# Indirect DMAs of 128 partitions in place of 125 in a two-layer graph network kernel

## The chip, the cores and the metric

One core of one Trainium2 chip. The metric is the device time of one execution in microseconds (us), the median of three runs.

## What is computed

Two layers on a graph of 12,500 nodes with 256 features and 212,500 edges, sorted by destination. The parts around the change are the two edge sums:

```
# layer 0: norm = dinv[src] * w * dinv[dst]
agg = segment_sum(norm[:, None] * h[src], dst, num_segments=12500)
# layer 1, with source and destination in exchanged roles
out = segment_sum(edge_vals[:, None] * seq_fts[edge_col], edge_row, num_segments=12500)
```

In both, each edge fetches a row of 256 floats (1 KB) by one end's index and adds it, weighted, to the row of the other end. Layer 1 sums by source, so the edges have to be put into another order first: every edge becomes a record of three words (12 B) and is written to its place in an array `sorted_recs`. Around the sums stand a linear attention, a mixture of eight experts (layer 0), a second attention with a feed-forward part and a slice attention (layer 1).

## The kernel before

Nodes are taken in 100 tiles of P = 125, edges in 1700 rows of 125. A plan stage (`plan`, L181) lays the edges of a layer out in 1800 steps of up to 125 edges, all of one tile; `k.src_p`, `k.dloc_p` and `k.w_p` hold for every step, one lane (partition) per edge, the row to fetch, the place in the tile and the weight. The plan fetches edge rows with indirect DMAs of its own, 120 lanes each (L288), and turns them with TensorE.

The edge sum is the class `Aggregation` (L840), used by `sum_layer0` (L959) and `sum_layer1` (L2046). Each layer goes through 25 supertiles of STEPS = 72 steps, in groups of GRP = 6. Per step:

- GpSimd (POOL) issues one indirect DMA, L885, that gathers 125 rows of 1 KB, one to a partition, into one of RING = 18 buffers (three groups). Before a group it waits until TensorE has finished the group three before (L881). Twice in a supertile it copies 36 columns of indices into `idx` (L873).
- VectorE builds a 125x125 matrix from place and weight, L916.
- TensorE multiplies matrix by rows, L950, into one of three PSUM buffers. It waits once per group for the six gathers (L946).
- VectorE adds the result to `k.sums`, L935.

Every engine runs its own instruction list in order; semaphores join them. Other work of a layer is written by hand into the same lists, between half groups of three steps: in layer 0 the keys of the attention and the ranks of the edges for the later order (DVE L1050, PE L1118, L1126); in layer 1 the attention and the feed-forward part. In layer 1 POOL also computes the two reciprocal roots of a supertile (`rstd`, L2155 and L2158), one ahead of the gathers of group 3, one ahead of those of group 7 (L2165 to L2168); each waits for VectorE's mean and variance.

`finish_layer0` (L1270) goes through 50 pairs of tiles. TensorE runs 32 slots of expert products per pair with the rest of the layer between them; POOL issues the scatter of the records, 34 indirect DMAs of 125 lanes x 12 B per pair (L1456), in four shares between four rstds (L1438, L1441), the last share of 17 ahead of the next pair's first rstd, which VectorE waits for at L1544. SP loads records and positions for the scatter from DRAM (L1415, L1416) and waits before for the scatters of an earlier pair (L1414).

POOL runs with no other queue for these DMAs: gathers and scatters, copies of indices and rstds stand in one list.

Of the kernel before, what the change touches and what calls it, by code (L numbers as in the profile page):

```python
# [23 lines left out]

P = 125
TS = 4
D = 256
# [153 lines left out]
def plan(nc, k, layer):  # L181
# [10 lines left out]
    with ExitStack() as ctx:  # L192
# [100 lines left out]
        def _(eng):  # L293
# [7 lines left out]

            eng.memset(ones[:], 1.0).then_inc(ones_done, 1)
            link(eng.memset(k.dloc_p[:, NS:], -1.0))
            link(eng.memset(k.w_p[:, NS:], 0.0))
# [52 lines left out]
            for g in range(NG):  # L357
                eng.wait_ge(edges_in[g], 16 * len(fetches))
                if g >= 2:

                    eng.wait_ge(turned, g - 1)
                eng.tensor_copy(src_f[:, g % 2, :], src_g[:, g, :])
                eng.tensor_copy(w_f[:, g % 2, :], w_g[:, g, :])
                eng.tensor_scalar(dst_f[:, g % 2, :], dst_g[:, g, :], ntile_col[:, g:g + 1], None, ALU.add)\
                   .then_inc(edges_f, 1)
                eng.wait_ge(turned, g + 1)
                for n, out in enumerate((k.src_p, k.dloc_p, k.w_p)):
                    eng.tensor_copy(out[:, g * SG:(g + 1) * SG], ps_t[0:P, n, (g % 2) * 256:(g % 2) * 256 + SG])\
                       .then_inc(laid, 1)
# [470 lines left out]
class Aggregation:  # L840
# [8 lines left out]
    def __init__(self, nc, k, sb, pb, sem, table):  # L849
        self.nc, self.k, self.table = nc, k, table  # L850
        self.idx = [sb(f"idx{n}", [P, STEPS // 2], I32) for n in range(2)]
        self.rows = sb("gathered", [P, self.RING, D])
        self.lay = sb("lay", [P, 2, GRP, P])
# [87 lines left out]
    def multiply(self, i, g, half):  # L941
# [5 lines left out]
        for l in range(half * GRP // 2, (half + 1) * GRP // 2):  # L947
            s = g * GRP + l
            eng.wait_ge(self.added, i * STEPS + s + 1)
            eng.matmul(self.res[s % self.RES][:, 0, :], self.lay[:, g % 2, l, :],  # L950
                       self.rows[:, s % self.RING, :], start=True, stop=True).then_inc(self.multiplied, 1)

# [317 lines left out]
def finish_layer0(nc, k):  # L1270
# [11 lines left out]
    with ExitStack() as ctx:  # L1282
# [42 lines left out]
        rs = sb("rstds", [P, 4, TE])  # L1325
        rec = sb("rec", [P, 2, RPP, 3], I32)
        pos = sb("pos", [P, 2, RPP], I32)
        ps_up = [pb(f"ps_up{n}", [128, TE * P]) for n in range(2)]
# [10 lines left out]
        x_in = [sem(f"x_in{j}") for j in range(TE)]  # L1339
        rec_in = [sem(f"rec_in{n}") for n in range(2)]  # L1340
        scattered = [sem(f"scattered{n}") for n in range(2)]
        out_done = [sem(f"out_done{j}") for j in range(TE)]
# [35 lines left out]
        def _(eng):  # L1378
# [24 lines left out]
            def run(i, n, turn, front=True, moe=True, back=True):  # L1403
# [7 lines left out]
                if moe:  # L1411

                    if not isinstance(i, int) or i > 0:
                        eng.wait_ge(S.share_done, i)  # L1414
                    eng.dma_start(rec[:, n, :, :], k.rec_d[:, bass.ds(i * RPP, RPP), :]).then_inc(rec_in[n], 16)  # L1415
                    eng.dma_start(pos[:, n, :], k.pos_d[:, bass.ds(i * RPP, RPP)]).then_inc(rec_in[n], 16)  # L1416
                if back:
# [11 lines left out]
        def _(eng):  # L1429
            eng.memset(neg_half[:], -0.5).then_inc(S.power_ready, 1)  # L1430
            eng.wait_ge(S.power_ready, 1)
            eng.sem_inc(S.share_done, 1)
# [1603 lines left out]
def whole(nc, **t):  # L3036
# [16 lines left out]
    with ExitStack() as ctx:  # L3053
# [13 lines left out]
        k.pos_d = nc.dram_tensor("pos_d", [P, k.ROWS], I32, kind="Internal").ap()  # L3067
        k.sorted_recs = nc.dram_tensor("sorted_recs", [E, 3], I32, kind="Internal").ap()
        k.sorted_rows = k.sorted_recs.rearrange("(r e) f -> r (e f)", e=P)

# [42 lines left out]
def step_lists(k, sb):  # L3113
    k.src_p = sb("src_p", [P, k.NS], I32)
    k.dloc_p = sb("dloc_p", [P, k.NS + GRP])
# [30 lines left out]
```

## Time and profile before

| | |
|---|---|
| median of 3 runs | 11389.68 us (11383.44 to 11391.83) |
| profiled execution: span | 11392.9 us, 3.2 us above the median |
| TensorE (PE) busy | 8144.0 us, 71% |
| POOL busy | 7159.8 us, 63% |
| VectorE (DVE) busy | 6467.8 us, 57% |
| mean granted TensorE clock | 0.795 of full |

The profile gives no time of its own for the profiled execution beside the span, from its first instruction to its last. Busy time does not hold register, branch, semaphore and DMA-issuing work of an engine's sequencer; for POOL's indirect DMAs the time in which it makes them is shown as busy, the time between two of them as idle, with "issue" as the releaser where nothing was waited for. An average over the span says little here, since the stages have different limits; the profile is cut at them below.

### The profile page before, as it was taken

Reading aid. Unit: us, or ns where it says so; the run is one execution under the profiler, and the core shown is the slowest. Engines: PE = TensorE matmul, PEld = TensorE weight load, DVE = VectorE, ACT = ScalarE, POOL = GpSimd, SP = SyncE. Lnnn points to the kernel's source line nnn. Section 1 sums busy time; section 2 is a strip of 40 time slices with the busy share of each in tenths; the row PEclk is TensorE's granted clock in tenths of the full one; section 3 lists DMA queues with packets and bytes.
Section 4 is the critical chain, followed back from the end, with each engine's and each line's share of the span. In section 5 each row is a group of like instructions: output and inputs, shape, how many; then the busy total and the mean of one; then the engine's idle time right before and its main releaser. Section 6 shows DMA issues by size and latency. Waiting matters only on the chain. (4 is left out here: it accounts for less than half of the span.)

```text
span 11392.9 us, 139911 instructions
## 1 busy us (share of the span) xinstructions
PE 8144.0 (71%) x33573; PEld 5854.9 (51%) x33573; DVE 6467.8 (57%) x21682; ACT 1705.4 (15%) x3275; POOL 7159.8 (63%) x6381
## 2 busy tenths in 40 slices
PE   4633666666666688888888876777778777777778
PEld 3422444444444466666666654545545455444446
DVE  5853666666666555555555545566665665544431
ACT  0000000000000133333333330000101000011100
POOL 2224777777777577777777776777777777500001
PEclk7656777787787788888888876888878888777779
DMA  1013333333333211111111113333333333222224
GB/s 44 23 48 98 87 90 88 90 88 90 90 88 90 51 17 17 16 16 16 16 16 16 16 15 86 86 87 86 86 88 86 88 86 86 72 64 62 63 75 140
DMA packets 751763, 731.65 MB, mean 64 GB/s; under 512 B 422416, under 2 KB 612397, under 8 KB 750777
## 3 DMA queue, kind: packets, MB, share of 16 engines
q0 software_dynamic: 529008, 487.89, 19.0%
q1 hardware_dynamic: 209539, 224.42, 6.3%
q10 hardware_dynamic: 12755, 15.35, 0.4%
q14 instruction: 436, 3.57, 0.1%
q8 instruction: 25, 0.41, 0.0%
HBM read 613.00 MB, written 108.35 MB: 63 GB/s over the span
## 5 line engine op out<-in xcount | busy, mean ns | idle before, releaser
L885 POOL DMA_INDIRECT sum_gathered<-table,sum_idx x3600 | 4403.9, 1223 | 1159.5 <-issue 1019.3
L950 PE MATMUL sum_agg_res<-sum_gathered,sum_lay 125*125 125x256 f32 x7200 | 2443.1, 485 | 1571.3 <-DMA sum_gathered<-table,sum_idx 964.1
L950 PEld LDWEIGHTS sum_agg_res<-sum_gathered,sum_lay 125*125 125x125 f32 x7200 | 1604.7, 237 | 2185.7 <-issue 1092.0
L1456 POOL DMA_INDIRECT sorted_recs<-fin_rec,fin_pos x1700 | 2117.7, 1246 | 504.0 <-issue 499.7
L935 DVE TENSOR_TENSOR all_sums<-all_sums,sum_agg_res 125x256 f32 x3600 | 1513.8, 421 | 1517.4 <-PE sum_agg_res L950 1364.7
L916 DVE TENSOR_SCALAR sum_lay<-all_lane,sum_dloc_now,sum_w_now 125x125 f32<-125x125 f32 x3612 | 1444.0, 403 | 20.8 <-DVE sum_xn_tiles L1067 17.3
L1887 PE MATMUL fin_ps_up<-fin_tokens_T,fin_w 128*128 128x250 f32 x3200 | 995.1, 447 | 0.0
L1895 PE MATMUL fin_ps_dn<-fin_w,fin_hidden 128*125 128x256 f32 x3200 | 860.3, 404 | 10.2 <-issue 10.0
L1887 PEld LDWEIGHTS fin_ps_up<-fin_tokens_T,fin_w 128*128 128x128 f32 x3200 | 695.9, 231 | 166.6 <-issue 69.2
L1525 DVE SCALAR_TENSOR_TENSOR fin_acc<-fin_ps_dn,fin_comb,fin_acc 125x256 f32<-125x256 f32 x800 | 381.3, 482 | 573.9 <-PE fin_ps_dn L1895 558.6
L1895 PEld LDWEIGHTS fin_ps_dn<-fin_w,fin_hidden 128*125 128x125 f32 x3200 | 600.8, 197 | 127.6 <-issue 49.4
L2616 POOL TENSOR_SCALAR slices_var_eps<-slices_mean_var 125x2 f32<-125x2 f32 x50 | 11.0, 219 | 944.9 <-DVE slices_mean_var L2656 931.6
L1760 ACT ACTIVATE fin_hidden<-fin_ps_up,fin_b 128x250 f32<-128x250 f32 x800 | 376.4, 471 | 934.8 <-PE fin_ps_up L1887 806.9
L2361 PE MATMUL sum_ps_C<-sum_x_T,sum_w 128*128 128x500 f32 x800 | 387.5, 608 | 0.0
L2375 PE MATMUL sum_ps_A<-sum_w,sum_low 128*125 128x256 f32 x1600 | 378.0, 379 | 0.0
L2375 PEld LDWEIGHTS sum_ps_A<-sum_w,sum_low 128*125 128x125 f32 x1600 | 300.1, 188 | 116.1 <-issue 80.8
L1050 DVE CUSTOM_DVE_ANT_0 sum_junk<-sum_src_hot,sum_ps_rank 125x100 f32<-125x100 bf16 x1700 | 335.6, 254 | 9.1 <-PE sum_ps_rank L1118 8.5
L514 DVE TENSOR_SCALAR deg_hot<-deg_lane,deg_dloc_now 125x128 bf16<-125x128 bf16 x1800 | 306.1, 251 | 7.9 <-DVE deg_xn_tiles L551 7.9
L1040 DVE TENSOR_TENSOR sum_src_hot<-sum_lane,steps_src_tile 125x400 bf16<-125x400 bf16 x425 | 243.3, 572 | 98.7 <-PE sum_ps_rank L1126 89.7
L1099 ACT COPY sum_xnT<-sum_ps_T 128x250 f32<-128x250 f32 x100 | 36.9, 369 | 1661.2 <-PE sum_ps_T L1145 1607.9
L2307 ACT ACTIVATE sum_low<-sum_ps_C,sum_b 128x500 f32<-128x500 f32 x200 | 135.5, 678 | 836.1 <-PE sum_ps_C L2361 771.7
L2977 POOL DMA_DIRECT2D out_x<-out_res x50 | 57.8, 1156 | 303.1 <-DVE out_res L2999 285.1
(480 smaller groups left out, 11713.0 us busy)
## 6 DMA issues: line engine op xcount, KB each, us to landing
sum_gathered<-table,sum_idx POOLq DMA_INDIRECT x3600
sorted_recs<-fin_rec,fin_pos POOLq DMA_INDIRECT x1700
slice_weights<-slices_sw SPq DMA_DIRECT2D x50, 500.0 KB
out_sw<-slice_weights SPq DMA_DIRECT2D x50, 500.0 KB
deg_x_tiles<-in_x SPq DMA_DIRECT2D x100, 125.0 KB
table_c_x<-in_x SPq DMA_DIRECT2D x25, 500.0 KB
table<-table_c_x ACTq DMA_DIRECT2D x25, 500.0 KB
sum_x_tiles<-in_x SPq DMA_DIRECT2D x100, 125.0 KB
```

The lines of the kernel that those rows point to most:

```text
L885: eng.indirect_dma_start(out=self.rows[:, s % self.RING, :], out_offset=None, in_=self.table, in_offset=bass.IndirectOffsetOnAxis(ap=self. ...
L916: ins = eng.tensor_scalar(self.lay[:, g % 2, l, :], k.lane[0:P, 0:P], self.dl[:, s:s + 1], self.wl[:, s:s + 1], ALU.is_equal, ALU.mult)
L935: eng.tensor_tensor(sums, sums, res, ALU.add).then_inc(self.added, 1)
L950: eng.matmul(self.res[s % self.RES][:, 0, :], self.lay[:, g % 2, l, :], self.rows[:, s % self.RING, :], start=True, stop=True).then_inc(se ...
L1050: ins = eng.tensor_tensor_reduce(junk[:, q, :], hot[:, slot(b), q, :], ps_rank[:, q, :], 1.0, 0.0, ALU.mult, ALU.add, rank[:, b * 4 + q:b ...
L1456: eng.indirect_dma_start(out=k.sorted_recs, out_offset=bass.IndirectOffsetOnAxis(ap=pos[:, n, r:r + 1], axis=0), in_=rec[:, n, r, :], in_o ...
L1525: eng.scalar_tensor_tensor(out=acc[:, n, j, :], in0=ps_dn[j][:, :], scalar=comb[:, n, j, e:e + 1], in1=acc[:, n, j, :], op0=ALU.mult, op1= ...
L1760: eng.activation(hid[:, e % 2, c, :], ps_up[c][:, :], ACT.Gelu, bias=b1[:, c, e:e + 1])\
L1887: mm = eng.matmul(ps_up[c][:, :], w1[:, e, m, c * H2:(c + 1) * H2], xtT[:, n, m, :, :], start=(m == 0), stop=(m == 1))
L1895: mm = eng.matmul(ps_dn[j][:, :], hid[:, e % 2, m, j * P:(j + 1) * P], w2[:, e, m, :], start=(m == 0), stop=(m == 1))
L2361: mm = eng.matmul(ps_C[u % 2][:, 0:T], w1[:, m, u * 128:(u + 1) * 128], xT[:, m, :], start=(m == 0), stop=(m == 1))
L2375: mm = eng.matmul(ps_A[j // 2][0:P, (j % 2) * D:(j % 2 + 1) * D], hid[:, u % 2, j * P:(j + 1) * P], w2[:, u, :], start=False, stop=False, ...
```

## The change

Every gather of the two edge sums and every scatter of the records has LANES = 128 lanes. `k.src_p`, the index buffers and the gather buffers get 128 partitions; lanes 125 to 127 of the indices are zero, so they fetch row 0 of the table, and TensorE reads lanes 0 to 124 only. The records' buffer and the positions get 128 partitions too; POOL sets the records' buffer to zero and fills the positions' spare lanes with places behind the last record, each written by one lane only; `sorted_recs` is longer by 2 x 34 x 3 = 204 records. SP's loads fill lanes 0 to 124 and the first waits for POOL's fills.

```diff
 P = 125
+LANES = 128
...
             eng.memset(ones[:], 1.0).then_inc(ones_done, 1)
+            link(eng.memset(k.src_p[:, :], 0))
             link(eng.memset(k.dloc_p[:, NS:], -1.0))
...
-                for n, out in enumerate((k.src_p, k.dloc_p, k.w_p)):
+                for n, out in enumerate((k.src_p[0:P, :], k.dloc_p, k.w_p)):
...
-        self.idx = [sb(f"idx{n}", [P, STEPS // 2], I32) for n in range(2)]
-        self.rows = sb("gathered", [P, self.RING, D])
+        self.idx = [sb(f"idx{n}", [LANES, STEPS // 2], I32) for n in range(2)]
+        self.rows = sb("gathered", [LANES, self.RING, D])
...
-                       self.rows[:, s % self.RING, :], start=True, stop=True).then_inc(self.multiplied, 1)
+                       self.rows[0:P, s % self.RING, :], start=True, stop=True).then_inc(self.multiplied, 1)
...
-        rec = sb("rec", [P, 2, RPP, 3], I32)
-        pos = sb("pos", [P, 2, RPP], I32)
+        rec = sb("rec", [LANES, 2, RPP, 3], I32)
+        pos = sb("pos", [LANES, 2, RPP], I32)
+        spare = LANES - P
...
                         eng.wait_ge(S.share_done, i)
-                    eng.dma_start(rec[:, n, :, :], k.rec_d[:, bass.ds(i * RPP, RPP), :]).then_inc(rec_in[n], 16)
-                    eng.dma_start(pos[:, n, :], k.pos_d[:, bass.ds(i * RPP, RPP)]).then_inc(rec_in[n], 16)
+                    else:
+                        eng.wait_ge(spare_ready, 3)
+                    eng.dma_start(rec[0:P, n, :, :], k.rec_d[:, bass.ds(i * RPP, RPP), :]).then_inc(rec_in[n], 16)
+                    eng.dma_start(pos[0:P, n, :], k.pos_d[:, bass.ds(i * RPP, RPP)]).then_inc(rec_in[n], 16)
...
             eng.memset(neg_half[:], -0.5).then_inc(S.power_ready, 1)
+            eng.memset(rec[:, :, :, :], 0).then_inc(spare_ready, 1)
+            for n in range(2):
+                eng.iota(pos[:, n, :], [[spare, RPP]], base=P * k.ROWS + n * RPP * spare - P, channel_multiplier=1)\
+                   .then_inc(spare_ready, 1)
...
-        k.sorted_recs = nc.dram_tensor("sorted_recs", [E, 3], I32, kind="Internal").ap()
-        k.sorted_rows = k.sorted_recs.rearrange("(r e) f -> r (e f)", e=P)
+        spare_recs = 2 * (k.ROWS // (k.NT // 2)) * (LANES - P)
+        k.sorted_recs = nc.dram_tensor("sorted_recs", [E + spare_recs, 3], I32, kind="Internal").ap()
+        k.sorted_rows = k.sorted_recs[0:E, :].rearrange("(r e) f -> r (e f)", e=P)
...
-    k.src_p = sb("src_p", [P, k.NS], I32)
+    k.src_p = sb("src_p", [LANES, k.NS], I32)
```

## Rows read from the trace of the kernel before

**Rows 1.** The page, part 5: line, engine, op, names, count | busy us, mean ns | idle before.
```profile
L885 POOL DMA_INDIRECT sum_gathered<-table,sum_idx x3600 | 4403.9, 1223 | 1159.5 <-issue 1019.3
...
L1456 POOL DMA_INDIRECT sorted_recs<-fin_rec,fin_pos x1700 | 2117.7, 1246 | 504.0 <-issue 499.7
```

**Rows 2.** Windows: busy us (instructions) per engine, TensorE clock, DMA share, GB/s.
```profile
993.00:3771.00 2778.00, 1722.11 (x7948) 1329.89 (x7949) 1838.87 (x7657) 78.09 (x199) 2197.13 (x1846) 0.80 0.36 89
...
3850.00:6830.00 2980.00, 2536.78 (x10282) 1937.29 (x10282) 1587.22 (x5374) 1118.37 (x2188) 2315.54 (x2100) 0.85 0.13 16
...
6940.00:9895.00 2955.00, 2285.45 (x7200) 1507.71 (x7200) 1800.72 (x4585) 271.83 (x440) 2259.07 (x1924) 0.82 0.34 86
```

**Rows 3.** Groups of POOL, 993 to 3771 us; columns as in rows 1.
```profile
L885 POOL DMA_INDIRECT sum_gathered<-table,sum_idx x1797 | 2186.6, 1217 | 581.0 <-issue 507.7 <-PE sum_agg_res L950 46.0 <-POOL sum_idx L873 27.3
```

**Rows 4.** Waits of TensorE, 1000 to 3770 us: us in total, times, longest.
```profile
PE sum_agg_res L950 <- DMA sum_gathered<-table,sum_idx: 805.8, 247, 9.0
```

**Rows 5.** Waits, all engines, 6890 to 9900 us.
```profile
PE sum_agg_res L950 <- DMA sum_gathered<-table,sum_idx: 151.9, 38, 8.2
...
POOL sum_var_eps L2155 <- DVE sum_mean_var L2185: 116.4, 25, 6.4
```

**Rows 6.** Waits, all engines, 3860 to 6790 us.
```profile
POOL sorted_recs L1456 <- issue: 495.8, 1673, 0.3
DVE fin_next_norm L1544 <- POOL fin_rstds L1441: 259.4, 49, 8.2
...
POOL fin_var_eps L1438 <- DVE fin_mean_var L1510: 101.5, 32, 16.4
```

**Rows 7.** Waits of TensorE, 3860 to 6790 us.
```profile
PE fin_ps_M L1922 <- DVE fin_gcn L1569: 9.7, 13, 1.7
```

**Rows 8.** Timeline of POOL, layer 0: start, length, instruction, idle before.
```profile
3764.42 1.21 POOL L885 DMA_INDIRECT sum_gathered<-table,sum_idx  x1 [0.30 <-issue]
...
3774.98 1.20 POOL L885 DMA_INDIRECT sum_gathered<-table,sum_idx  x1 [0.30 <-issue]
```

**Rows 9.** Timeline of POOL, plan of layer 0.
```profile
82.68 1.00 POOL L288 DMA_INDIRECT plan_src_g<-in_src,plan_row_i  x1 [15.98 <-DVE plan_row_i L351]
...
85.27 0.98 POOL L288 DMA_INDIRECT plan_w_g<-in_edge_weight,plan_row_i  x1 [0.31 <-issue]
...
91.68 0.98 POOL L288 DMA_INDIRECT plan_dst_g<-in_dst,plan_row_i  x1 [0.31 <-issue]
```

**Rows 10.** Line L288: duration ns min/median/max, first and last start.
```profile
L288 POOL DMA_INDIRECT plan_rec_g<-sorted_recs,plan_row_i x15: 980/984/1107, 6863.2 to 6881.4; - x15
```

**Rows 11.** Line L885, 1000 to 3770 us; columns as in rows 10.
```profile
L885 POOL DMA_INDIRECT sum_gathered<-table,sum_idx x1792: 1196/1202/1607, 999.7 to 3769.0; - x200
```

**Rows 12.** DMA view, 82 to 142 us (45 indirect DMAs of the plan).
```profile
DMA packets 1441, 2.71 MB, mean 45 GB/s; under 512 B 765, under 2 KB 765, under 8 KB 1440
```

**Rows 13.** DMA view, 2000 to 2300 us.
```profile
DMA packets 26821, 26.93 MB, mean 90 GB/s; under 512 B 18493, under 2 KB 20964, under 8 KB 26801
...
q0 software_dynamic: 24851, 25.13, 33.9%
...
sum_gathered<-table,sum_idx POOLq DMA_INDIRECT x196
```

**Rows 14.** Timeline of POOL, layer 1.
```profile
7573.82 0.23 POOL L2155 TENSOR_SCALAR sum_var_eps<-sum_mean_var 125x4 f32<-125x4 f32 x1 [5.95 <-DVE sum_mean_var L2185]
...
7583.19 1.55 POOL L885 DMA_INDIRECT sum_gathered<-table,sum_idx  x1 [0.30 <-issue]
```

**Rows 15.** Timeline of TensorE, layer 1.
```profile
7587.80 2.92 PE L950 MATMUL sum_agg_res<-sum_gathered,sum_lay 125*125 125x256 f32 x6 [3.65 <-DMA sum_gathered<-table,sum_idx]
```

**Rows 16.** Timeline of VectorE, plan of layer 0.
```profile
87.97 0.23 DVE L362 CAST plan_src_f<-plan_src_g 120x125 f32<-120x125 int32 x1 [1.02 <-DMA plan_w_g<-in_edge_weight,plan_row_i]
```

**Rows 17.** Timeline of VectorE, plan of layer 1.
```profile
6850.52 0.22 DVE L306 TENSOR_SCALAR plan_tri_ge<-plan_diff 101x101 f32<-101x101 f32 x1 [2.01 <-POOL plan_step_of L274]
...
6854.27 1.16 DVE L346 TENSOR_SCALAR plan_reached<-plan_step_row,plan_start 101x1800 f32<-101x1800 f32 x1
```

More of the change, by code:

```diff
@@ L1340, in finish_layer0 @@
         rec_in = [sem(f"rec_in{n}") for n in range(2)]
+        spare_ready = sem("spare_ready")
         scattered = [sem(f"scattered{n}") for n in range(2)]
```

## The prediction

> **What bounds the kernel now.** I read the groups of instructions first. GpSimd (POOL) issues 3600 gathers and 1700 scatters, 1223 and 1246 ns each on average, 6.52 ms of an 11.39 ms span, and most of its idle time before them is "issue", about 0.30 us before each, where it waits for nobody [rows 1]. Then I cut the span at the stages [rows 2]: the layer 0 edge sum (993 to 3771), the finish of layer 0 with the scatter (3850 to 6830), the layer 1 edge sum (6940 to 9895). One stage at a time:
>
> Layer 0 sum: the 1797 gathers seen there took 2186.6 us and the idle time before them 581.0 us; together 2767.6 of the 2778 us, so POOL does nothing but issue gathers back to back [rows 3]. TensorE is late only because of them: it waited 805.8 us for gathered rows [rows 4]. The price of a gather on POOL sets this stage.
>
> Layer 1 sum: POOL is not alone. Once in each of the 25 supertiles it stands still for a mean and variance of VectorE, 116.4 us in all, 4.7 each, and TensorE waits for gathered rows only 151.9 us in all, 6.1 per supertile [rows 5]. TensorE is busy 2285 of 2955 us; the rest of its idle time is the back and forth with VectorE.
>
> Finish: POOL is nearly full, 2315.5 us busy and 495.8 of issue in 2980 us, 94%; of the 59.6 us of each of the 50 pairs of tiles, its 34 scatters take 34 x (1.246 + 0.296) = 52.4 [rows 1, 2, 6]. VectorE waits for POOL's rstd at L1544, 259.4 us in 49 times, 5.3 each, yet TensorE waits at the place behind it (L1922, for VectorE's gcn) only 9.7 us in all [rows 7]; it is busy 2537 of 2980 us. So TensorE and the router's chain set the pair, not the scatters.
>
> **The price of 128 lanes.** No row shows an indirect DMA of 128 lanes. In the sum, eight 125-lane gathers start 10.56 us apart from first to last, a pitch of 1.509 us [rows 8]. The plan stage has indirect DMAs of 120 lanes: eight start 9.00 us apart, a pitch of 1.286 us, each 0.98 us long [rows 9]. Five lanes more cost 0.223 us, 23%; so the price is not proportional to lanes. Nor is it bytes: the 125-lane scatter moves 12 B a lane and costs as much as the gather with 1024 B, and the 120-lane fetch of records, 1500 B a lane, costs 984 ns [rows 1, 10]. What differs is how the lanes are spread: 45 DMAs of 120 lanes left 1441 packets, 32 each, of which (1441 - 765)/45 = 15 are large, 4000 B, that is eight rows in each of 15 streams [rows 12]. 196 gathers of 125 lanes left 24851 packets, 127 each, and (26801 - 20964)/196 = 30 large ones: six packets of four rows (and one row over) in each of five streams of 25 [rows 13]. 125 divides only by 5 up to 16; 120 by 15, 128 by 16. With 16 streams of eight rows a 128-lane DMA is, stream for stream, the 120-lane one. I take its price, 1.286. The ends for the range: proportional to lanes from there, 0.98 x 128/120 = 1.045, pitch 1.35; or on the line through 120 and 125 lanes, (1.202 - 0.98)/5 = 0.044 us a lane, 1.335, pitch 1.64 [rows 9, 11] (a rival below).
>
> The Trainium skill, DMA: Bandwidth & Descriptors, section on why a DMA increments its semaphore by 16, gives the rule: the largest count of engines up to 16 that divides the partitions. Its other section, Anatomy of one DMA (SWDGE path), speaks against this change: descriptor generation is called small, with many descriptors emitted before a cost shows. By that 128 lanes would cost POOL what 125 do and the layer 0 term below would be nil. The rows with 0.98 and 1.20 us disagree with it.
>
> **The change part by part**, against the span of 11392.9 us; the three runs have a median 3.2 us lower, so I take differences and subtract them from 11389.7.
> 1. Layer 0 sum: 1800 gathers x 0.223 = 401 us less, if TensorE and VectorE keep up. A supertile takes 2778/25 = 111.1 us; without its 32.2 us of waiting for rows TensorE would need 78.9 [rows 2, 4], VectorE is busy 73.6, and POOL will need 111.1 - 72 x 0.223 = 95.1. POOL stays last. -401.
> 2. Layer 1 sum: POOL becomes 16 us per supertile faster and mostly waits longer for the mean and variance, since the rstd of half-way stands ahead of the seventh group of gathers. What is on the path is the chain behind that wait: rstd at 7573.82, six gathers, the last starting at 7583.19 and taking 1.55, and TensorE's matmul at 7587.80 after 3.65 us of idleness for the rows [rows 14, 15]. Six gathers give 6 x 0.223 = 1.3. Landing: here 3.06 us from the last issue's end to the matmul; behind the 120-lane fetch of 85.27, which ends at 86.25, VectorE starts at 87.97, 1.72 later [rows 9, 16]. So 1.3 more. 25 x 2.6 = 65 us. The other, shorter wait for rows (the third group after the start of a supertile) I cost at nothing: VectorE's two 3.3 us reciprocals follow and cover it. Bounds: 0 and the whole 151.9. -65.
> 3. Finish: 34 scatters x 0.223 = 7.6 us less on POOL per pair. The rstds come earlier, VectorE's 5.3 us wait at L1544 goes, but what it holds up on TensorE is 9.7 us in all. With a little for the other rstds I take -15. Bounds: 0, and 5.3 x 49 = 260.
> 4. Dummy lanes: 2.4% more bytes, on engines a third busy [rows 2]. Three reads of one table row per gather and three 12 B writes to spare rows are hidden behind POOL's pitch. 0, at worst a few tenths in the landing, times 25.
> 5. Setup: a memset of 128x1800 on VectorE in each plan. A pass over 101x1800 took 1.16 us, and VectorE then sat 2.01 us waiting for POOL's constants [rows 17], which hides it; 0, at worst 2 x 1.2. One memset and two iotas on POOL ahead of the first scatter: under 1 us, where POOL has nothing else to do until the first statistics come. SP's first load of records now waits for them; it stands behind 27 weight loads and a wait for VectorE on SP's queue, so nothing queued behind it is late. 0.
> Sum: -401 - 65 - 15 = -481, 11390 - 481, about **10910 us**.
>
> **Rivals.**
> A. The forecast. Own range 10780 to 11030: the low end takes 150 in layer 1 and 60 in the finish; the high end the pitch 1.35, 1800 x 0.16 = 288, and 25 x 2.
> B. Slower: price by the line. If POOL's time rises with every lane beyond 120, 128 lanes cost 0.133 more than 125. Layer 0: +239. Layer 1: 72 x 0.133 = 9.6, less 4.7 of slack, x 25 = +123. Finish: 34 x 0.133 = 4.5, less the 2 us per pair that POOL still waits (101.5 us in all [rows 6]), x 50 = +125. 11880. It decides as soon as a gather's own time is above 1.20. For: two points make a line. Against: it would be 44 ns a lane where 120 lanes cost 8 each.
> C. No price change: 128 lanes cost POOL 1.20 as 125 do, and only the landing in layer 1 shortens, 25 x 1.3 = 33: 11357, or 11390 without that. The Trainium skill's remark on descriptor generation, DMA: Bandwidth & Descriptors, amounts to this. Against: the packets.
> D. Layer 0's other engines become last: TensorE and VectorE pass three results between them in fixed order, and some of the waiting for rows may come back as waiting for sums. Half of term 1 lost: 11110. Against: VectorE's waits there are of TensorE, which in turn waits for rows.
> E. The finish was bound by POOL after all (94% taken), and VectorE's 5.3 us come off the pair: a further 245 us, 10665. For: POOL is fuller than any engine. Against: 9.7 us.
>
> **How the numbers follow.** A 0.73, E 0.08, D 0.08, C 0.06, B 0.05. Predicted: A, 10910. A and D hold 0.81: the range goes from 10700, where A with term 2 at its bound of 152 and 85 in the finish ends (11390 - 401 - 152 - 85 = 10752, and 50 for a higher TensorE clock where its waits go), to 11110. About 0.2% (23 us) is what a measurement can tell from no change. Faster: A, D, E and a third of C, 0.91. Same: the rest of C, 0.04. Slower: B, 0.05.
>
> **What would show it.** Right: gathers and scatters near 0.98 us with 0.30 of issue; 48 packets per gather, 32 of them large; the layer 0 stage near 2377 us with POOL still back to back; POOL's wait at L2155 grown from 4.7 towards 18 us per supertile; VectorE's wait at L1544 nearly gone and the finish near 2965. Wrong: a 128-lane gather at 1.2 us or more (C, B); in layer 0, POOL waiting for TensorE at L885 (D); the finish 200 us shorter (E).

## The result, and the profile after

Slower: 12379 us (median of 4 runs, 12366 to 12431) against 11391 (11383 to 11405), a ratio of 1.0872 with a 95% interval of 1.0849 to 1.0895. I had forecast 10910. The profiled execution spans 12429.9 us, 1037 more than before.

The groups of instructions of the changed kernel, the lines that answer to [rows 1] and two more (busy us, mean ns | idle time before them, and what ended it):

```profile
L887 POOL DMA_INDIRECT sum_gathered<-table,sum_idx x3600 | 3498.0, 972 | 2261.4 <-PE sum_agg_res L952 1072.5 <-issue 996.4 <-remote 180.5
...
L1466 POOL DMA_INDIRECT sorted_recs<-fin_rec,fin_pos x1700 | 1709.6, 1006 | 497.6 <-issue 497.2 <-DVE fin_mean_var L1520 0.3
...
L1052 DVE CUSTOM_DVE_ANT_0 sum_junk<-sum_src_hot,sum_ps_rank 125x100 f32<-125x100 bf16 x1700 | 335.9, 253 | 280.5 <-DMA plan_w_g<-in_edge_weight,plan_row_i 259.4 <-issue 11.0 <-PE sum_ps_rank L1120 9.6
...
L1042 DVE TENSOR_TENSOR sum_src_hot<-sum_lane,steps_src_tile 125x400 bf16<-125x400 bf16 x425 | 243.3, 572 | 281.7 <-DMA plan_w_g<-in_edge_weight,plan_row_i 186.5 <-PE sum_ps_rank L1128 53.5 <-issue 37.0
```

Both kinds of DMA became about as cheap as forecast (near 0.98 us): 0.97 and 1.01 us, 1314 us of POOL's time saved. Their pitch, the time from the start of one to the start of the next, is 1.25 and 1.26 us, a little under the 1.286 of the forecast. And yet all three stages take longer. VectorE's lines at L1042 and L1052 now stand idle for 446 us until "DMA plan_w_g", a transfer that was issued hundreds of microseconds earlier (the last one at 139 us): the trace finds nobody who released them. In the kernel before these two lines stood idle for 107 us, nearly all of it for TensorE. Such a false releaser is the first thing to see here.

The stages of the changed kernel, from the first to the last indirect DMA of each (columns as in [rows 2]):

```profile
993.00:4040.00 3047.00, 1859.36 (x7945) 1337.70 (x7943) 1807.85 (x7641) 78.00 (x199) 1748.00 (x1849) 0.73 0.28 82
4121.00:7659.00 3538.00, 2511.13 (x10149) 1908.54 (x10150) 1569.50 (x5333) 1105.96 (x2164) 1892.88 (x2092) 0.80 0.06 13
7785.00:10920.00 3135.00, 2322.00 (x7211) 1494.24 (x7212) 1771.40 (x4609) 274.76 (x445) 1833.70 (x1947) 0.81 0.29 84
```

and of the kernel before, cut in the same way:

```profile
993.00:3775.00 2782.00, 1726.11 (x7959) 1333.09 (x7960) 1840.88 (x7663) 78.09 (x199) 2200.22 (x1849) 0.80 0.36 89
3854.00:6803.00 2949.00, 2520.61 (x10240) 1927.15 (x10240) 1579.18 (x5352) 1114.31 (x2179) 2305.67 (x2092) 0.85 0.13 16
6904.00:9892.00 2988.00, 2296.73 (x7238) 1515.49 (x7239) 1811.93 (x4623) 275.81 (x447) 2286.64 (x1946) 0.82 0.34 87
```

Layer 0's sum grew by 266 us, the finish by 589, layer 1's sum by 147; the rest (35) lies between the stages and behind them. VectorE is no busier in any of them. TensorE is busier by 133 us in layer 0, where its granted clock fell from 0.80 to 0.73 of full speed, and by 25 in layer 1. So most of what each stage grew by is idle time, not work. Whose? The finish shows it best. VectorE's router chain (it picks the experts of the pair's tokens) is some twenty tiny instructions, most of which wait on VectorE's own semaphore for one ahead. Before, lines from its middle (start, us, ...; x2 is one instruction for each tile of the pair, timed from the start of the first to the end of the second):

```profile
4554.30 0.68 DVE L1679 CAST fin_top_f<-fin_top_i 125x2 f32<-125x2 uint32 x2
4554.53 0.66 DVE L1681 TENSOR_TENSOR fin_gate<-fin_top 125x1 f32<-125x1 f32 x2
4555.12 0.27 DVE L1683 TENSOR_SCALAR fin_gate<-fin_gate 125x1 f32<-125x1 f32 x2
```

and the same instructions after, while POOL issues the last 17 scatters of the pair:

```profile
4744.99 0.17 DVE L1689 CAST fin_top_f<-fin_top_i 125x2 f32<-125x2 uint32 x1 [0.57 <-DVE fin_top_f L1689]
4745.66 0.16 DVE L1691 TENSOR_TENSOR fin_gate<-fin_top 125x1 f32<-125x1 f32 x1 [0.50 <-DVE fin_top_f L1689]
4746.38 0.18 DVE L1691 TENSOR_TENSOR fin_gate<-fin_top 125x1 f32<-125x1 f32 x1 [0.57 <-issue]
4747.09 0.15 DVE L1693 TENSOR_SCALAR fin_gate<-fin_gate 125x1 f32<-125x1 f32 x1 [0.53 <-issue]
4748.44 0.15 DVE L1693 TENSOR_SCALAR fin_gate<-fin_gate 125x1 f32<-125x1 f32 x1 [1.20 <-issue]
```

None of these instructions takes longer than before (now 0.15 to 0.18 us), but 0.5 to 1.2 us pass until the next one starts: VectorE's own semaphore increments come back late. Over the whole finish the mean gap between an instruction of VectorE and the next one, where that waits for its semaphore, is 0.192 us (0.019 before; where the two overlap, the gap counts as negative). TensorE waits for this chain's last result, its longest wait in the finish (us in total, times, longest):

```profile
PE fin_ps_T L2019 <- DVE fin_comb L1706: 562.1, 46, 16.1
```

TensorE's 562 us at that one place were 150.9 in the kernel before; the 411 more stand against the stage's 589. In layer 1's sum POOL's wait for the mean and variance (L2165) grew from the 116.4 us of [rows 5] to 301.6.

In layer 0 the increments are TensorE's, and later still. All engines there, between two groups of gathers:

```profile
2002.77 0.38 PE L1128 MATMUL sum_ps_rank<-sum_src_hot,sum_edges_after 125*125 125x100 bf16 x4
...
2006.33 0.42 DVE L937 TENSOR_TENSOR all_sums<-all_sums,sum_agg_res 125x256 f32 x1 [2.15 <-remote]
...
2007.66 0.94 POOL L887 DMA_INDIRECT sum_gathered<-table,sum_idx  x1 [0.30 <-issue]
...
2008.90 0.94 POOL L887 DMA_INDIRECT sum_gathered<-table,sum_idx  x1 [0.30 <-issue]
2011.99 0.57 DVE L1042 TENSOR_TENSOR sum_src_hot<-sum_lane,steps_src_tile 125x400 bf16<-125x400 bf16 x1 [5.25 <-DMA plan_w_g<-in_edge_weight,plan_row_i]
...
2012.81 0.94 POOL L887 DMA_INDIRECT sum_gathered<-table,sum_idx  x1 [2.96 <-remote]
```

L1042 waits for the last of the four matmuls of L1128, which ended at about 2003.15. It starts at 2011.99. The records of semaphore updates in the same trace say why (semaphore, what posts it, time of the update):

```
123  PE L1128 (rest_done)   2011.86
121  PE L1120 (pre_done)    2011.92
105  PE L952  (multiplied)  2006.19  2011.96  2012.00  2012.04
119  PE L1158 (ctx_done)    2012.10
```

TensorE's increments of more than six microseconds of work arrive together within 0.25 us, half a microsecond after the last data packet of POOL's last gather (2011.30). POOL, too, starts again only behind them: before a group it waits for the same `multiplied`, so that its ring of 18 tiles counted as full. I call this **late posts**: while indirect DMAs follow each other closely, increments by the engines wait, and in this stretch they come through when POOL pauses. As a measure for layer 0 I take the share of the updates of `multiplied` that follow the one before within 0.1 us, closer than two of these results can end, since each takes TensorE about 0.4 us and more: 0.00 before, 0.11 after. GpSimd's own posts are late too: between its copy of the indices (L875), for whose semaphore it waits, and the next gather lay 0.98 us in the mean in layer 0 before, and 2.3 after.

TensorE's granted clock is a mean of its two levels, 2.4 GHz (1.0) and 1.2 GHz (0.5). In layer 0 it stood at the lower one for 40% of the stage before and for 54% after.

### The profile page after: what moved, and what is told of

The parts are those of the page before. It is cut to its first block and busy times, and to the rows that moved or that the text cites. A ratio compares the mean times of both kernels' runs of the same rounds, so it can differ in the third digit from the quotient of the medians.

```text
span 12429.9 us, 139916 instructions
## 1 busy us (share of the span) xinstructions
PE 8327.2 (67%) x33573; PEld 5844.0 (47%) x33573; DVE 6404.8 (52%) x21684; ACT 1705.1 (14%) x3275; POOL 5842.2 (47%) x6384
## 5 line engine op out<-in xcount | busy, mean ns | idle before, releaser
L887 POOL DMA_INDIRECT sum_gathered<-table,sum_idx x3600 | 3498.0, 972 | 2261.4 <-PE sum_agg_res L952 1072.5
L952 PE MATMUL sum_agg_res<-sum_gathered,sum_lay 125*125 125x256 f32 x7200 | 2513.2, 490 | 1274.1 <-DVE all_sums L937 476.6
L1466 POOL DMA_INDIRECT sorted_recs<-fin_rec,fin_pos x1700 | 1709.6, 1006 | 497.6 <-issue 497.2
L918 DVE TENSOR_SCALAR sum_lay<-all_lane,sum_dloc_now,sum_w_now 125x125 f32<-125x125 f32 x3612 | 1277.5, 354 | 20.8 <-DVE sum_xn_tiles L1069 11.2
L1448 POOL TENSOR_SCALAR fin_var_eps<-fin_mean_var 125x2 f32<-125x2 f32 x200 | 44.2, 221 | 1193.9 <-DVE fin_mean_var L1520 1193.9
L1128 PE MATMUL sum_ps_rank<-sum_src_hot,sum_edges_after 125*125 125x100 bf16 x1700 | 209.0, 257 | 410.7 <-DVE sum_rank_now L1052 287.0
L1052 DVE CUSTOM_DVE_ANT_0 sum_junk<-sum_src_hot,sum_ps_rank 125x100 f32<-125x100 bf16 x1700 | 335.9, 253 | 280.5 <-DMA plan_w_g<-in_edge_weight,plan_row_i 259.4
L2019 PE MATMUL fin_ps_T<-all_ident,fin_comb 125*8 125x125 f32 x100 | 39.1, 391 | 607.8 <-DVE fin_comb L1706 562.1
L1128 PEld LDWEIGHTS sum_ps_rank<-sum_src_hot,sum_edges_after 125*125 125x125 bf16 x1700 | 191.3, 172 | 511.0 <-DVE sum_rank_now L1052 336.8
L1042 DVE TENSOR_TENSOR sum_src_hot<-sum_lane,steps_src_tile 125x400 bf16<-125x400 bf16 x425 | 243.3, 572 | 281.7 <-DMA plan_w_g<-in_edge_weight,plan_row_i 186.5
```

Of the source, the lines that this page charges most:

```text
L887: eng.indirect_dma_start(out=self.rows[:, s % self.RING, :], out_offset=None, in_=self.table, in_offset=bass.IndirectOffsetOnAxis(ap=self. ...
L918: ins = eng.tensor_scalar(self.lay[:, g % 2, l, :], k.lane[0:P, 0:P], self.dl[:, s:s + 1], self.wl[:, s:s + 1], ALU.is_equal, ALU.mult)
L1128: mm = eng.matmul(ps_rank[:, q, :], upper[:], hot[:, slot(b), q, :], start=False, stop=False, skip_group_check=True)
L1466: eng.indirect_dma_start(out=k.sorted_recs, out_offset=bass.IndirectOffsetOnAxis(ap=pos[:, n, r:r + 1], axis=0), in_=rec[:, n, r, :], in_o ...
```

## The experiments

The theories at the start: **L**, late posts are caused by the indirect DMAs as the change made them, through their shares, their rate or their dummy lanes; **P**, placement, the added instructions shifted some engine's code. The experiments stand in six groups, each on another chip and beside the kernel before, whose median was 11388 to 11416 in all six.

### Which part of the change

The whole change, but each indirect DMA back at 125 partitions:

```diff
-                out=self.rows[:, s % self.RING, :], out_offset=None, in_=self.table,
-                in_offset=bass.IndirectOffsetOnAxis(ap=self.idx[half][:, s - half * hs:s - half * hs + 1], axis=0))\
+                out=self.rows[0:P, s % self.RING, :], out_offset=None, in_=self.table,
+                in_offset=bass.IndirectOffsetOnAxis(ap=self.idx[half][0:P, s - half * hs:s - half * hs + 1], axis=0))\
...
-                            out=k.sorted_recs, out_offset=bass.IndirectOffsetOnAxis(ap=pos[:, n, r:r + 1], axis=0),
-                            in_=rec[:, n, r, :], in_offset=None).then_inc(scattered[n], 16)
+                            out=k.sorted_recs, out_offset=bass.IndirectOffsetOnAxis(ap=pos[0:P, n, r:r + 1], axis=0),
+                            in_=rec[0:P, n, r, :], in_offset=None).then_inc(scattered[n], 16)
```

> Keeps every addition of the change (tiles of 128 partitions, the memsets and the iotas, the wait for them, the longer record tensor) but gives each indirect DMA of the edge sums and of the record scatter its 125 partitions back. In the profiles of before and after, the three stages with these DMAs grew by 266, 589 and 147 us (first to last DMA: 2781 to 3047, 2949 to 3538, 2988 to 3135), although one DMA fell from 1.22 to 0.97 us. Theory L (late posts: with 128 partitions back to back, the semaphore increments of all engines arrive late): 11390, within 25. Theory P (placement: the added instructions shifted the code of some engine and it now fetches instructions at a worse moment; the partitions have nothing to do with it): about 12380, DMAs at 1.22 us and stages still long.

Measured: 11407 us, ratio 0.9992 (0.9983 to 1.0002). P is out, and the setup costs nothing that can be told from zero.

The same diff with its second part alone (gathers at 128), then with its first part alone (scatter at 128):

> The change for the gathers of the two edge sums alone; the record scatter has 125 partitions. Theory L: the stages of the edge sums keep their 266 and 147 us more, the finish stage goes back to some 2950 us, so 11390 + 266 + 147 + some 20 between the stages = 11820, between 11770 and 11880. Theory D (the three dummy lanes, which all read row 0 of the table, are what slows the gathers, and something else the scatter): no other time in this run; it is told apart later. Theory P: about 12380 as after.

Measured: 11771 us, 1.031 (1.0292 to 1.0327), +354. Stages 3002, 2957, 3124 us.

> The change for the record scatter alone; the gathers have 125 partitions. Theory L: only the finish stage grows, by 589 us: 11390 + 589 = 11980, between 11920 and 12030, with VectorE's waits for its own semaphore near 0.19 us in the mean in that stage (0.02 before) and the gathers at 1.22 us. If the scatter slowed by what it writes (the spare rows) and not by how many partitions it has, the time is the same here, and a later run has to tell it. Theory P: about 12380.

Measured: 12012 us, 1.0518 (1.0501 to 1.0536), +596. Stages 2791, 3552, 2980 us; VectorE's gap 0.195 us in the finish. The two add up to 950 of 988, and each does its harm in its own stage.

### Dummy lanes or not, and how many shares

A DMA of n partitions is cut into as many equal shares as the largest divisor of n up to 16, as the packets had shown for 120 and 125 [rows 12, 13]; for the other sizes I take it to be so. The first two of these runs have the first part of the diff above with `0:112` or `0:120` in place of `0:P`, the second part as it stands, and `self.rows` set to zero once. They leave out 13 or 5 rows of every step, and TensorE's instructions stay the same; the third is the whole change with

```diff
-LANES = 128
+LANES = 126
```

> Gathers of 112 partitions (no dummy lane; 13 of the 125 rows of every step of both edge sums are left out and stay zero), record scatter with 125. 112 is 16 times 7, so 16 equal shares as with 128. Compared with the run of 128-partition gathers alone (11771, +354 over before). Theory D (the three dummy lanes, all reading row 0, do the harm): the cheaper gathers pay as I forecast, about 10950. Theory L (the split over 16 queues, or the pitch that comes of it): late posts as with 128, 11600 to 11850.

> Gathers of 120 partitions (no dummy lane; 5 of the 125 rows of every step are left out and stay zero), record scatter with 125. 120 is 15 times 8: 15 shares, which the 120-partition DMAs of the plan had at 0.98 us. Theory L in its general form (many queues at a pitch under 1.3 us): 11600 to 11850, as with 112 and 128. Theory L16 (only the full 16 shares do it, one queue in particular being the one that posts go through): pitch 1.25 to 1.29 us without late posts, about 10950. Theory D: about 10950 as well, so the 112-partition run tells D from L16.

> The whole change with 126 partitions instead of 128, one dummy lane: 14 shares of 9, nothing left out. Theory L in its general form: late posts nearly as with 128, 12100 to 12400. Theory L16: DMA at about 1.0 us and no late posts, about 10950, which would beat both kernels. Theory D (harm in proportion to the dummy lanes): about 11390 + 1000/3 - 300 = 11400, between 11100 and 11700.

Measured: 112 partitions 11871 us, 1.0422 (1.0404 to 1.0439); 120 partitions 11669, 1.0234 (1.0215 to 1.0254); the whole change at 126, 12218, 1.0722 (1.0704 to 1.074). Without a dummy lane the loss is 468 and 266 us, against 354 for the gathers with 128: D is out. Fifteen and 14 shares do harm too, so L16 is out. Then an attempt to lengthen the pitch of the changed kernel, behind each gather, and the same behind each scatter:

```diff
+            eng.memset(self.pace[:, s:s + 1], 0.0)
```

> The changed kernel (128 partitions in gathers and scatters) with one small memset (125x1) by GpSimd behind each of the 5300 indirect DMAs, so that they follow each other at about 1.5 us as before, not at 1.25. Theory R (rate: each such DMA loads the path of the semaphore posts for a fixed time, and a queue grows only where they come faster than it drains): the three stages go back towards 2781, 2949 and 2988 us, 11390 to 11550 in all, and VectorE's waits for its own semaphore in the finish stage from 0.19 back to 0.02 to 0.05 us. Theory S (shape: the 16-way split holds posts up at any rate): 12300 to 12700, since the memsets come on top.

Measured: 12517 us, 1.0978 (1.096 to 1.0996), but the pitch stayed 1.251 us: the memset ran inside the 0.30 us that had looked like idle time. So it says nothing on R or S. Three memsets each:

> The changed kernel with three small memsets (125x1) by GpSimd behind each of the 5300 indirect DMAs. One such memset took 0.12 us and was hidden in the 0.30 us between two DMAs (the pitch stayed 1.251 us); three should push the pitch to 1.35 to 1.6 us, 10 to 12 shares in a us. Theory Q: at 10 to 11 in a us VectorE's waits for its own semaphore in the finish stage fall from 0.195 us to 0.17 (what the 126-partition run had) or below, and the time lies between 12000 and 12400, mending less than half. Theory by pitch alone: at a pitch of 1.5 us the waits are back at 0.02 to 0.05 us and the time at 11400 to 11600.

Measured: 12316 us, 1.0787 (1.0766 to 1.0809); they too hid, the pitch was 1.27 in the sums and 1.29 in the finish, with a gap of 0.148 us there. Neither theory was tested. On the same chip, gathers by turns and gathers of 100 partitions (`0:100` as above):

```diff
+            n = LANES if s % 2 else P
-                out=self.rows[:, s % self.RING, :], out_offset=None, in_=self.table,
+                out=self.rows[0:n, s % self.RING, :], out_offset=None, in_=self.table,
```

> Gathers of 125 and 128 partitions by turns (even and odd steps), record scatter with 125; nothing left out. So far layer 0's stage lasted, by shares and pitch of its gathers: 5 shares at 1.51 us 2781 us, 14 at 1.30 2951, 15 at 1.29 2964, 16 at 1.25 3002 to 3047: in the order of shares per time (3.3, 10.8, 11.7, 12.8 in a us). By turns it would be 10.5 shares in 1.38 us, 7.6 in a us. Theory Q (a path that the shares load, with a limit between 3.3 and 10.8 in a us): if the limit lies above 7.6, the posts stay prompt and both stages gain by the pitch, 1800 x 0.13 = 230 us in layer 0 and some 30 in layer 1, 11140 in all, and it would beat both kernels; if it lies below, between 11450 and 11700. Theory E (every 16-share DMA delays the posts behind it by itself, whatever the load): half the loss of 354 us, 11580.

Measured: 11433 us (11390 to 11466), 1.0024 (1.0009 to 1.0039), layer 0 at 2733 us, with late posts (0.08). To this I come back.

> Gathers of 100 partitions (25 of the 125 rows of every step are left out and stay zero), record scatter with 125. 100 is 10 times 10, so 10 equal shares of 10 rows at a pitch of about 1.31 us, 7.6 shares in a us. Theory Q: as the run by turns: under the limit 11000 to 11100 (layer 0's stage near 2450 to 2600 us), over it 11450 to 11650. Theory by pitch alone (what counts is that the gathers come faster than 1.5 us, in whatever shares): about as the 120-partition run, 11600 to 11700.

Measured: 11641 us, 1.0205 (1.0188 to 1.0222), layer 0 at 2936 us. Ten shares at 1.309 us do as much harm as 14 at 1.297 (2951). Theory Q, shares per time, would have put it with the run by turns, whose load is the same; it falls.

### Shares against frequency

`0:25` and `0:85` in the gathers as above, and the changed kernel with, behind each gather and in the same way behind each scatter,

```diff
+            eng.tensor_tensor(self.pace[:, s:s + 1], self.pin[:], self.pin[:], ALU.pow)
```

> Gathers of 25 partitions only (100 of the 125 rows of every step are left out and stay zero), record scatter with 125. 25 is 5 times 5: as few shares as with 125 partitions, but a pitch of some 1.2 us. Theory N (the number of shares decides): the posts stay prompt, the edge sums' stages are no longer held by GpSimd, time 10800 to 11050 as I had forecast for the change. Theory F (the frequency decides, whatever the shares: gathers that follow each other in under about 1.4 us make the posts late): 11600 to 11900, with waits of GpSimd for its own copy of the indices of 1.5 us and more in the mean (0.98 before).

> Gathers of 85 partitions (40 of the 125 rows of every step are left out and stay zero), record scatter with 125. 85 is 5 times 17: 5 shares again, between 25 and 125 partitions, pitch about 1.4 us. Theory N: posts prompt, layer 0's stage 1800 x 1.4 + 70 = 2590 us, time about 11150. Theory F: between the run by turns and that of 100 partitions, 11450 to 11600.

> The changed kernel with one pow on 125x1 by GpSimd (0.7 us each) behind each of the 5300 indirect DMAs, which cannot hide in the 0.30 us between two of them as the memsets did: pitch about 1.65 us with 128 partitions and 16 shares. Edge sums: 1800 x 1.65 + 70 = 3040 us for layer 0 and about 3230 for layer 1 from the pitch alone, so the time is not the measure here; the finish stage, where 34 such DMAs take 56 of 59 us, is, with the posts. Theory F: finish stage about 2950 to 3000 us, VectorE's waits for its own semaphore there 0.02 to 0.05 us (0.19 in the changed kernel), about 11900 in all. Theory N: the waits stay above 0.1 us and the finish stage above 3300, 12300 or more in all.

Measured: 25 partitions 11792 us, 1.0355 (1.0338 to 1.0372); 85 partitions 11356, 0.9965 (0.9951 to 0.9979); with the pow 12836, 1.1268 (1.1249 to 1.1287). Layer 0 with 25 partitions, POOL's waits and its window:

```profile
POOL sum_gathered L888 <- PE sum_agg_res L953: 606.9, 145, 17.4
```

```profile
999.00:4026.00 3027.00, 1843.09 (x7945) 1323.71 (x7944) 1797.44 (x7642) 78.05 (x199) 1728.90 (x1849) 0.74 0.08 20
```

A fifth of the rows, a quarter of the bytes (20 GB/s against 82), five shares, and the stage is as long as with 128 partitions, with POOL waiting for TensorE as in the changed kernel. With the pow, 16 shares at 1.785 us, the waits of layer 0 look as in the kernel before, where TensorE waits for rows, and POOL waits for no other engine:

```profile
PE sum_agg_res L956 <- DMA sum_gathered<-table,sum_idx: 1353.7, 281, 9.1
```

Late posts: 0.16 with 25 partitions, 0.08 with 85, 0.00 with the pow. GpSimd's wait for its own copy in layer 0: 2.11 us with 25 partitions, 0.87 with the pow. In the finish VectorE's gap with the pow was 0.028 us. The finish itself still took 3462 us: I had expected a pitch of 1.65, it was 1.83, and POOL alone was busy 3042 us of it. These three runs stand on one chip. So theory F holds and N falls: **how often indirect DMAs follow each other decides**, not what they move or in how many shares. Two limits of that: the pow changes more than the pitch, since POOL then runs something else between two DMAs; and every one of these DMAs adds 16 to its semaphore, so that no run tells the frequency of the issues from that of their increments. The runs of layer 0 so far, ordered by pitch:

```
partitions   shares  pitch us  layer 0 us  late posts
112          16      1.232     3027        0.14
25            5      1.241     3027        0.16
128          16      1.251     3002-3047   0.11-0.14
128+3 memset 16      1.27      3049        0.14
120          15      1.287     2964        0.12
126          14      1.297     2951        0.12
100          10      1.309     2936        0.13
125/128     5/16      1.38     2733        0.08   (and 2580, 0.00: below)
85            5      1.402     2743        0.08
125           5      1.51      2781-2791   0.00
128 + pow    16      1.785     3309        0.00
```

### Where the limit lies

128 partitions at every second, third or sixth step of layer 0 alone; all else at 125, nothing left out:

```diff
-            n = LANES if s % 2 else P
+            n = LANES if self.table is self.k.table0 and s % 3 == 2 else P
```

> Gathers of 128 partitions at every second step of layer 0's sum only; layer 1's gathers and the record scatter have 125, nothing is left out. In the run by turns layer 0's stage fell from 2781 to 2733 us while layer 1's grew from 2988 to 3033. Theory F (posts get late with the frequency of the indirect DMAs; about where the mean pitch falls under 1.4 us the loss eats the gain): layer 0 near 2733, the rest as before, 11350, a ratio of 0.996. If only disturbance between cases is at work: 11390.

> The same with 128 partitions at every third step of layer 0's sum: mean pitch 1.509 - 0.258 / 3 = 1.423 us. Theory F with a limit between 1.40 and 1.51 us: if the posts are still prompt at 1.42, layer 0's stage is 1800 x 0.086 = 155 us shorter, 11240; if the loss begins gradually, as the 85-partition run (1.402 us, 2743 us) suggests, near 2700 and 11310. In either case it should be the fastest of the kernels that leave nothing out, together with the next.

> The same with 128 partitions at every sixth step of layer 0's sum: mean pitch 1.509 - 0.258 / 6 = 1.466 us. Theory F: posts prompt (late ones under 2% of those of TensorE), layer 0's stage 1800 x 0.043 = 77 us shorter, 2704, and 11315 in all. If the harm came with every single 128-partition DMA instead of with the mean frequency, this run would gain nothing: 11390.

Measured: half 11176 us, 0.9814 (0.9801 to 0.9828); a third 11265, 0.9884 (0.9868 to 0.9899); a sixth 11326, 0.9944 (0.9931 to 0.9958). Layer 0's stages: 2579, 2644, 2717 us, no late posts in any. The third and the sixth came near their numbers for prompt posts, the half was 174 us better than expected. Its layer 0 has the very gathers of the run by turns, which had taken 2733 us. Both once more, together on one chip:

> The kernel with 128-partition gathers at every second step of layer 0 alone, a second time, together with the kernel that has them in both layers. The first time it was at 0.9814 of before, layer 0's stage 2579 us and no late posts; the kernel by turns in both layers has the very same layer 0, but took 2733 us for it, with late posts, in another call on another chip. Theory C (the limit lies a little differently from chip to chip or call to call; the two kernels behave alike in layer 0 on one chip): both layer 0 stages of this call within 20 us of each other, whether at 2580 or at 2730, so this kernel at 11180 or at 11350. Theory K (something in the kernels differs): this one again at 11180 with the other at 11430.

> The kernel with 125 and 128 partitions by turns in both layers, a second time, in one call with the kernel above. Theory C: layer 0's stage as above; if it is the prompt case, layer 1 is no longer than before either (2950 to 2990 us) and the time 11130 to 11190; if the late case, 11430 as the first time. Theory K: 11430 with layer 0 at 2730 while the kernel above has 2579.

Measured: half of layer 0 11189 us, 0.982 (0.9807 to 0.9834); by turns in both layers 11175, 0.9813 (0.98 to 0.9827). Both layer 0 stages took 2580 to 2584 us: theory C holds, and K is out. Layer 0 of the kernel by turns, in its first and in its second run:

```profile
994.00:3727.00 2733.00, 1757.65 (x7956) 1255.05 (x7955) 1817.82 (x7655) 78.06 (x199) 2001.01 (x1849) 0.77 0.34 91
```

```profile
987.00:3567.00 2580.00, 1673.70 (x7959) 1288.31 (x7958) 1822.07 (x7661) 78.07 (x199) 1994.53 (x1848) 0.81 0.37 97
```

The same instructions, POOL and VectorE equally busy, 153 us apart; TensorE is 84 us busier in the first, at a clock of 0.77 against 0.81. So in the last two groups the limit lies below 1.38 us. In the two groups before them it lies above 1.38 or 1.40, where posts were late, and in the first two above 1.25 or 1.30; the kernel before, at 1.51, kept its time in all. Whether the chip makes the difference or the time at which a group ran is not shown, since each group had a chip of its own. The whole change was not run in the last two. Whether it would be slow there is open; with posts prompt at 1.25 us my forecast might have come true.

One more difference goes with it. Each indirect DMA increments its semaphore 16 times, and the trace should hold 16 update records for it. In layer 0 (1000 to 3500 us) it holds 12.9 per gather before, 4.4 after, 5.1 with 25 partitions, 6.3 in the first run by turns, 12.4 with the pow, and 16.4 in the second run by turns (a few updates of other DMAs among them). Where records are lost most, posts are late; where none is lost, they are prompt. The loss does not go with the pitch alone: layer 1's gathers in the run with half of layer 0 are those of the kernel before, at the same 1.516 us, and kept 16.0 records each, where the kernel before kept 13.9 in layer 1. Of TensorE's increments of `multiplied` in layer 0 the kernel before shows 1539 of 1794, all five runs of the last two groups all but one or two. In whole executions the traces hold 53,600 updates after, 96,600 before and 121,500 in each of those five. So those two groups differ from the others in how well records get through, and also in how early posts get late. The records may be the cause, not only a witness: every execution here, the timed ones too, had its spans and clocks recorded. The Trainium skill, NOTIFIC — the notification-queue block, section on overflow, says that a full queue, in one of its modes, or a filled internal stage can hold up the engine that makes the records. No run here shows that, since none was made without records. If it is so, a part of the 8.7%, or all of it, is a cost of being recorded. It stays open.

One more rule bears on VectorE and GpSimd side by side: the Trainium skill, SBUF — State Buffer, section Who interferes with whom, says that VectorE in some of its modes and GpSimd lock each other out of a shared port. It does not explain what happened here: TensorE's posts were late as well, and the 0.15 us instructions of VectorE's router kept their length.

## Why the prediction was wrong

**The price: right.** I took the 1.286 us pitch of the 120-lane DMAs for 128 lanes; it was 1.251, and 48 packets per gather (8496 for 177 gathers between 2000 and 2300 us), as written. A gather of 25 partitions took 0.965 us and one of 85 took 1.13, so the count of rows per share matters, as argued from [rows 12, 13]. Rivals B and C fell with that.

**Step 1, layer 0: the step that failed.** "-401. POOL stays last." It was +266, 667 of the 1469 us between forecast and result, and POOL stood waiting for TensorE for 635.4 us of the stage. TensorE's 78.9 us per supertile were worked out as its present time less its wait for rows, which takes for granted that no other wait changes. What I left out was not an engine: it is the delivery of everybody's semaphore increments, which was held up beside the tighter series of indirect DMAs. Where posts were prompt, the reasoning of this step held. Half of the gathers at 128 partitions should have given half of 401; the second run by turns gave 2781 - 2580 = 201; a third and a sixth of them gave 137 and 64, where 134 and 67 were due.

**Step 2, layer 1: wrong sign.** -65 forecast, +147 measured, with POOL waiting 301.6 us for the mean and variance (116.4 in [rows 5]) and 437 us for TensorE. The change of gathers alone gives 136 of it. Even with prompt posts this term was too large: the second run by turns had half of these gathers at 128 and a layer 1 of 2976 us, against 2982 for 125 throughout on the same chip, where half of 65 less was due.

**Step 3, the finish: wrong, and the largest loss of a stage.** -15 with bounds of 0 and -260; it was +589. I had read rightly that TensorE and the router's chain set the pair and not the scatters, and concluded that scatters can't matter to it. They do: the chain is some twenty posts long, and in the stretch shown, while POOL scattered, each came 0.5 us or more later. It was the place with the most to lose, and I gave it no bound on that side.

**Steps 4 and 5, dummy lanes and setup.** The setup is right at nothing (ratio 0.9992). That the dummy lanes cost nothing fits: 112 partitions without any were no faster than 128.

**Rival D** named the sign that came (POOL waiting for TensorE at the gathers, 1072.5 us), but for another reason and with a gain still left. My only slower case, B at 0.05, was POOL's own price; none had another engine or its posts suffer. The trace did hold a warning: the plan's 120-lane DMAs were the only indirect DMAs with a pitch under 1.5 us, and the edge sums and the finish, with their many semaphores, never ran beside such a pitch. The forecast moved 5300 DMAs into a region that no row covered, and bounded only their own cost there.

## What to carry to other kernels

A cheaper instruction that comes more often can cost others more than it saves. Before shortening the pitch of a long series of indirect DMAs, look for chains of short semaphore waits beside it; afterwards look for idle time whose releaser makes no sense (a transfer long over, "issue" in front of small instructions that used to follow each other directly), and try the change on a part of the series first. Here 128 partitions on every second gather of layer 0 took 1.9% off on two chips, and on every second gather of both layers 1.9% on one chip and nothing on another (1.0024), so measure such a gain on more than one chip.

## What was not expected of the hardware

- While indirect DMAs were issued at a pitch of 1.25 us, an increment by TensorE arrived 8.7 us late (due at 2003.15, there at 2011.86), those by VectorE in the stretch shown half a microsecond and more, GpSimd's own 1.3 us in the mean; those of the DMAs themselves went on arriving at that pitch. At 1.51 us no late post was seen, at 1.38 it differed between chips. Whether this is so without the recording of a profile is open.
- The pitch of an indirect DMA goes with the rows per share, hardly with the shares: 5 rows 1.24, 7 rows 1.23, 8 rows 1.25 to 1.29, 9 rows 1.30, 10 rows 1.31, 17 rows 1.40, 25 rows 1.51 us.
- One small memset of 0.12 us between two indirect DMAs left their pitch at 1.251 us: it fits in the 0.30 us that the trace calls "issue".
- TensorE's granted clock was lower where it had more idle time: 0.80 before and 0.73 after in layer 0, and for the very same instructions 0.77 in the 2733 us stage against 0.81 in the 2580 us one. The same work then took 133 and 84 us more of busy time.
